# A gather kernel on one core: four gathers a round cut short by 1, 2, 4 and 9 rows, SyncE fetching the rows left over

## The reference

```
h    = relu(layernorm(x))
cat  = concatenate(h[src], h[dst], edge_attr)          # E x 384
msg  = relu(cat @ W1 + b1)                             # W1: 384 x 128
aggr = segment_sum(msg, dst, N)
out  = x + layernorm(aggr + h) * gamma + beta
```

## Time and profile before

| | |
|---|---|
| median of three runs | 1979.93 us |
| profiled execution | 1981.21 us |
| its span, first to last instruction | 1979.4 us |
| busy: PE, GpSimd (POOL), ACT, DVE | 1568.1, 1486.8, 1315.3, 860.4 us |
| mean granted TensorE clock, as a share of 2.4 GHz | 0.903 |
| data moved | 305.82 MB, 155 GB/s |

### The profile page before, as it was taken

One profiled execution on the slowest core, in us unless ns is written; L12 is line 12 of the kernel. 1 busy time (PEld: TensorE's weight loads), 2 busy tenths in 40 slices (PEclk: granted clock), 3 DMA queues, 4 the chain that ended last, 5 costly groups with the idle time before them and its releaser, 6 DMA issues.

```text
span 1979.4 us, 51290 instructions
## 1 busy us (share of the span) xinstructions
PE 1568.1 (79%) x11881; PEld 1485.0 (75%) x11881; DVE 860.4 (43%) x3031; ACT 1315.3 (66%) x2288; POOL 1486.8 (75%) x1575
## 2 busy tenths in 40 slices
PE   5677888878888887888888778888878787877876
PEld 4577787877777787777777777778777677777766
DVE  6534444444444444444444444444344343434434
ACT  5566767667676666767676676767666676666655
POOL 7777777777777777777777777777777777777775
PEclk9888988889898888998888899889899998999998
DMA  9744645555454555555555555555555555555553
GB/s 247 203 135 141 172 139 162 151 154 158 141 171 143 160 155 148 166 139 165 148 155 157 147 166 144 158 154 157 152 146 151 149 150 151 158 146 151 145 158 86
DMA packets 244448, 305.82 MB, mean 155 GB/s; under 512 B 50892, under 2 KB 143540, under 8 KB 244420
## 3 DMA queue, kind: packets, MB, share of 16 engines
q1 hardware_dynamic: 168596, 192.06, 31.9%
q0 software_dynamic: 50048, 102.60, 20.4%
q10 hardware_dynamic: 25776, 10.86, 1.9%
HBM read 281.68 MB, written 23.64 MB: 154 GB/s over the span
## 4 chain that ended last, share of the span: by engine, by line
POOL 30%; issue 23%; DMA 20%; PE 13%; DVEq 7%; DVE 4%; POOLq 1%; ACT 1%; ACTq 0%
POOL a_rows L524 27%; DMA a_rows<-table_a,picks 20%; DVEq L1225 5%; PE ps_pre L678 4%; PE ps_pre L679 4%; POOL aggr L500 3%; PE ps_edge L665 2%; DVE msg L1221 2%; PE ps_sum L690 1%; PE ps_sum L697 1%; DVEq L1218 1%; DVE e_norm L1253 1%; ACT space L894 0%; DVEq L1220 0%; PE ps_fin L690 0%
## 5 line engine op out<-in xcount | busy, mean ns | idle before, releaser
L524 POOL DMA_INDIRECT a_rows<-table_a,picks x1500 | 1417.1, 945 | 457.0 <-issue 402.5
L678 PE MATMUL ps_pre<-w_c,edge_cols 128*128 128x128 f32 x3128 | 680.6, 303 | 60.2 <-issue 39.6
L679 PE MATMUL ps_pre<-b_win,onehot_cols 128*128 128x128 f32 x3128 | 670.7, 300 | 0.0
L1221 DVE TENSOR_TENSOR msg<-ps_pre,a_rows 128x512 f32<-128x512 f32 x391 | 270.2, 691 | 874.1 <-DMA a_rows<-table_a,picks 640.3
L907 ACT ACTIVATE msg<-msg 128x512 f32<-128x512 f32 x391 | 246.2, 630 | 603.1 <-DVE msg L1221 587.0
L678 PEld LDWEIGHTS ps_pre<-w_c,edge_cols 128*128 128x128 f32 x3128 | 538.8, 216 | 83.5 <-ACT edge_cols L900 63.3
L679 PEld LDWEIGHTS ps_pre<-b_win,onehot_cols 128*128 128x128 f32 x3128 | 540.2, 216 | 0.0
L894 ACT ACTIVATE space<-space,base_all 64x512 f32<-64x512 int32 x391 | 474.1, 1213 | 13.3 <-issue 10.1
L690 PE MATMUL ps_sum<-onehot,msg 128*128 128x64 f32 x1568 | 225.2, 291 | 105.8 <-ACT e_rows L925 54.9
L690 PEld LDWEIGHTS ps_sum<-onehot,msg 128*128 128x128 f32 x1568 | 212.5, 210 | 125.0 <-ACT e_rows L925 65.5
L902 ACT ACTIVATE onehot_cols<-space,ones 64x512 f32<-64x512 f32 x391 | 277.4, 709 | 0.0
(11 more groups left out here) (123 smaller groups left out, 1032.8 us busy)
## 6 DMA issues: line engine op xcount, KB each, us to landing
edges<-in_edge_attr SPq DMA_DIRECT2D x391, 256.0 KB
space<-in_dst SPq DMA_DIRECT2D x391, 128.0 KB
a_rows<-table_a,picks POOLq DMA_INDIRECT x1500
b_win<-table_b SPq DMA_DIRECT2D x391, 32.0 KB
out<-out_rows SPq DMA_DIRECT2D x97, 64.0 KB
table_b<-b_rows ACTq DMA_DIRECT2D x96, 64.0 KB
x_all<-in_x SPq DMA_DIRECT2D x13, 448.0 KB, 6.8
table_a<-a_out SPq DMA_DIRECT2D x13, 448.0 KB
```

Of the source, the lines that this page charges most:

```text
L524: pool.indirect_dma_start(a_rows[:, u, k, :], None, table_a[:, :], bass.IndirectOffsetOnAxis(ap=picks[:, u, k:k + 1], axis=0),).then_inc(s ...
L678: pe.matmul(to, edge_cols[:, u % 2, k * P:(k + 1) * P], w_c[:, :], start=True, stop=False)
L679: mm = pe.matmul(to, onehot_cols[:, u % 2, k * P:(k + 1) * P], b_win[:, u, :], start=False, stop=True)
L1221: dve.tensor_tensor(msg[:, u % 2, :, :].rearrange("p k f -> p (k f)"), ps_pre[u % 2][:, :], a_rows[:, u, :, :].rearrange("p k f -> p (k f) ...
```

## The change

In the first group of each round (u = 0) the four gathers take the first 127, 126, 124 and 119 partitions in place of 128. The 1 + 2 + 4 + 9 = 16 rows left over are fetched by SyncE, each with a transfer of one row of 512 B from table_a whose row number stands in a register. The row numbers are loaded from src into hand_ids in the first phase (round r in partition r), DVE copies them by the four places into hand_picks (16 numbers a round, one partition per round), and SyncE reads them into eight registers at a time (BATCH): eight behind the loads of the round's first group, eight behind those of its second. Ahead of the first eight it waits for the add of the first group of the round before, which frees a_rows[:, 0]. DVE's add of the first group waits for the 16 rows by a semaphore of their own. The second branch of the kernel isn't touched.

```diff
+GATHERED = (127, 126, 124, 119)
+BATCH = 8
...
+    HAND_FROM = min(GATHERED)
+    HAND_AT = [(p, k) for k in range(SUB) for p in range(GATHERED[k], P)]
+    HAND = len(HAND_AT)
...
             load_ids(0, src)
+            sp.dma_start(hand_ids[0:ROUNDS - 1, :, :],
+                         src[0:(ROUNDS - 1) * UNROLL * GROUP].rearrange(
+                             "(r e) -> r e", r=ROUNDS - 1)[:, HAND_FROM * SUB:GROUP].rearrange(
+                             "r (p k) -> r p k", k=SUB)).then_inc(s_hand_ids, 16)
...
+                def fetch(i, batch):
+                    _, rows = nc.values_load_multi_w_load_instructions(
+                        bass.at_runtime_partition(hand_picks[0:1, batch * BATCH:(batch + 1) * BATCH], i),
+                        [mybir.EngineType.SP], min_val=0, max_val=N - 1, skip_runtime_bounds_check_because="src holds node numbers")
+                    for n in range(BATCH):
+                        p, k = HAND_AT[batch * BATCH + n]
+                        sp.dma_start(a_rows[p:p + 1, 0, k, :], table_a[bass.ds(rows[n], 1), :]
+                                     ).then_inc(s_hand_rows, 16)
+
+                def fetches(i, u):
+                    if u == 0 and past(i, 1):
+                        sp.wait_ge(s_z, (i - 1) * UNROLL + 1)
+                    if u < HAND // BATCH:
+                        fetch(i, u)
+
+                sp.wait_ge(s_hand_picks, SUB)
                 for i in range(3):
                     for u in range(UNROLL):
                         step(i, u)
+                        fetches(i, u)
 
                 def round_(i):
                     for u in range(UNROLL):
                         step(i, u)
+                        fetches(i, u)
                     sp.wait_ge(s_out, i - 2)
...
                     for k in range(SUB):
+                        n = GATHERED[k] if u == 0 else P
                         pool.indirect_dma_start(
-                            a_rows[:, u, k, :], None, table_a[:, :],
-                            bass.IndirectOffsetOnAxis(ap=picks[:, u, k:k + 1], axis=0),
+                            a_rows[0:n, u, k, :], None, table_a[:, :],
+                            bass.IndirectOffsetOnAxis(ap=picks[0:n, u, k:k + 1], axis=0),
                         ).then_inc(s_a_rows[u][k], 16)
...
+            dve.wait_ge(s_hand_ids, 32)
+            at = 0
+            for k in range(SUB):
+                n = P - GATHERED[k]
+                dve.tensor_copy(hand_picks[0:ROUNDS, at:at + n],
+                                hand_ids[0:ROUNDS, GATHERED[k] - HAND_FROM:, k]).then_inc(s_hand_picks, 1)
+                at += n
...
+                    if u == 0:
+                        dve.wait_ge(s_hand_rows, (i + 1) * (HAND * 16))
```

More of the change, by code:

```diff
@@ L154, in build @@
         b_rows = sb("b_rows", [P, H])
+        hand_ids = sb("hand_ids", [P, P - HAND_FROM, SUB], I32)
+        hand_picks = sb("hand_picks", [P, HAND], I32)
         early_picks = sb("early_picks", [P, EARLY_GROUPS, SUB], I32)
@@ L269, in build @@
         s_first_picks = sem("s_first_picks")
+        s_hand_ids = sem("s_hand_ids")
+        s_hand_picks = sem("s_hand_picks")
+        s_hand_rows = sem("s_hand_rows")
         s_early_picks = sem("s_early_picks")
@@ L388, in _ @@
             load_ids(0, src)
+            sp.dma_start(hand_ids[0:ROUNDS - 1, :, :],
+                         src[0:(ROUNDS - 1) * UNROLL * GROUP].rearrange(
+                             "(r e) -> r e", r=ROUNDS - 1)[:, HAND_FROM * SUB:GROUP].rearrange(
+                             "r (p k) -> r p k", k=SUB)).then_inc(s_hand_ids, 16)
+            last = (ROUNDS - 1) * UNROLL * GROUP
+            sp.dma_start(hand_ids[ROUNDS - 1:ROUNDS, :, :],
+                         src[last + HAND_FROM * SUB:last + GROUP].rearrange("(o p k) -> o p k", o=1, k=SUB)
+                         ).then_inc(s_hand_ids, 16)
             with sp.Fori(0, CHUNKS // 2 - 1 - X_LEAD) as pair:
@@ L455, in _ @@
                     step(ROUNDS - 1, u)
+                    fetches(ROUNDS - 1, u)
                 for b in range(ROUNDS - 4, BLOCKS):
```

## The result

The changed kernel takes **2215.68 us** (median of four runs, 2210.56 to 2218.13); the kernel before, beside it, 1979.86 us (four runs). The ratio is 1.119, 95% interval 1.1175 to 1.1203: 236 us slower. The forecast was 2167 us, slower by SyncE. What follows is of the profiled execution, 2210.56 us with a span of 2208.7.

What follows compares the result with a forecast made beforehand. GpSimd's gathers were taken as the bound; SyncE, with 7.1 us free a round and 9.2 added, would take over. Start 76.3, unrolled rounds 56.4, 94 rounds 2000.3, then the tail: 2166.1 span, forecast 2167 us, range 1962 to 2450.

Steps and rivals of the forecast that it cites:

- What bounds the kernel, and SyncE's room: Main loop: GpSimd's gathers run end to end, 1873 of 1979 us; SyncE has 7.1 us of each round to give.
- Sixteen fetches: SyncE's one-row transfers: 0.48 us each, 7.7 us a round, or 0.66 and 10.6 with b_win's issue.
- Loads of eight registers: SyncE's two row-number loads: 0.45 us for the instruction, 0.76 a load, 1.5 a round; bounds 1.2 and 4.9.
- one by one: Rival on SyncE's register loads: each register costs a full 0.268 us, 12.6 us a round, 2495 us; chance 0.10 (2390 to 2495).
- the sum: SyncE's round: 12.1 us of old work plus 9.2 of new makes 21.3, giving 2167 us for the kernel.
- The landing and the wait for the add: Arrival of shortened gathers, 2 to 3 us late inside 5.2 spare, and SyncE's wait for DVE's add: both cost nothing.
- The shortened gathers: GpSimd's 392 gathers with fewer rows: time goes by rows, saving 11.6 us; bounds nothing to 15.3 us.
- the rule on divisors: Gathers' landing: a transfer uses the largest number of engines up to 16 dividing its slowest dimension; the sum stays the same.
- The bound against: GpSimd's shortened gathers: an odd shape could cost at most 0.12 us more each, 47 us over 392 gathers.
- odd sizes cost more: Rival on GpSimd: odd gather sizes cost more than the rows save, SyncE keeping up; 2027 us, chance 0.05.
- SyncE binds, GpSimd wants 19.06: Main loop: SyncE becomes the bound at 21.3 us a round where GpSimd needs only 19.06.
- the likeliest case's own range: Whole kernel: SyncE binds with register loads near one trip, 2100 to 2230 us; chance 0.38.

Runs made afterwards that it cites:

- e6: The change with 8 rows a round: one gather of 120 rows, the others 128, one batch of eight fetches; 1988.39 us, ratio 1.0049.
- e8b: Kernel before, plus eight rows a round fetched into memory for 64 rounds, and four whole gathers left out in round 64; 1986.20 us, ratio 1.0035.
- e5: The change with all 16 fetched rows taken from one gather of 112 rows, the other three 128; 2171.81 us, ratio 1.0975.
- e2b: Kernel before with gathers of 127, 126, 124 and 119 rows and nothing fetched; 2192.61 us, ratio 1.1078.

## Why the prediction was right and where it was wrong

*What bounds the kernel, and SyncE's room.* Right. GpSimd end to end, and SyncE has 7.1 us a round to give: e6, with one batch, stays inside it; e8b, with 7.25 us, just doesn't.

*Sixteen fetches.* 0.48 us each was predicted, 0.42 measured ((3.17 - 0.225) / 7). L360's 0.286 us was the right neighbour and still too dear; the issue is 0.225. Two batches with their loads were to add 9.2 us. The block from b_win's start to the next edges is 4.89 and 4.77 us where it was 0.82: 8.0 together.

*Loads of eight registers.* 0.45 us was taken for the instruction, 0.552 measured. One register takes 0.268, so each of seven more adds (0.552 - 0.268) / 7 = 0.04 us. The rival "one by one" (2495 us) is out, and with it, for a load from SBUF, the 200 ns a register of the Trainium skill's "Runtime: NRT & Kernel Launch", section "Instruction fetch mechanics".

*What the sum lacked on SyncE:* the load of b_win's row number behind a batch takes 0.605 us in place of 0.268 (L438's median; half of its loads stand in a group that follows fetches), twice a round 0.3 us. That makes 8.7 us in place of 9.2. The predicted round was 21.3, e5's 21.24; predicted 2167 us, e5 2171.8. **As a forecast for SyncE's half the sum is right to 5 us**, with errors of half a microsecond a round that cancel: without the 8.7, e5's round has 12.5 us where the walk of a round gave 12.1. In the round shown above, for instance, the fourth group up to the next round's edges takes 3.93 us where the sum had 3.71.

*The landing and the wait for the add.* Right in the main: e2b's GpSimd has no stop at all, so no landing held up a gather; DVE waits 436 us for gathered rows where it waited 640 before. The wait for the add was put at nothing and is 18.8 us.

*The shortened gathers: the step that failed.* It said -0.12 us a round, by rows; measured are +2.13 (+2.17 with the two gathers behind). Two things were wrong. That a gather's time goes by rows: 64 rows cost what 128 do within 0.04 us, so there was no saving to be had from any cut. And the rule on divisors was applied to the landing alone: "by that rule the sum stays the same". It was taken for granted that GpSimd's own 0.945 us has nothing to do with how the transfer is split, though the trace had only sizes of 128 and so could not say. The bound against, 0.12 us a gather, was taken from L500, whose gathers all have 128 rows, so that their higher mean isn't a matter of size; the real price was 0.53 on the mean, over four times the bound. The rival "odd sizes cost more" (2027 us, chance 0.05) was the right mechanism with a price too low by far. Priced rightly it would have stood at 2193, beside the forecast.

*Where the two meet.* The forecast of 2167 came out 49 us low: e5, SyncE alone, is 2172; e2b, GpSimd alone, is 2193; both together 2216. So the step "SyncE binds, GpSimd wants 19.06" put its figure on the lower one of two bounds that stand close together: up to 1885 us GpSimd sets the pace, and only the last 17.6 us (23 by the medians) are SyncE's. The result lies in the likeliest case's own range (2100 to 2230) in part by luck: of the 209 us that were missing all but 44 are hidden, as they run beside SyncE's work.

*Signs that were named.* "Gathers of 127 rows far from 0.945 us" was listed among those that would show the prediction wrong, and it is what the trace has (2.55), as "SyncE rounds of about 21.3 without a hole" is there on the other side. "GpSimd with gaps over 0.30 us", named as a sign of being right, is there seven times only: that is the mark of the wrong bound.

*The clock.* The mean granted TensorE clock is 0.851 where it was 0.903, and PE is busy for 77 us longer. Nothing in the prediction spoke of it, and it is no rival for the cause: the gathers run with their 0.30 us gaps up to 1885 us, so up to there no wait for PE held them up.

## What to carry to other kernels

An indirect gather has a price per instruction, and rows left out of it save next to nothing. Keep its rows a multiple of 16, and save on it only by having fewer of them. By the pitches measured, 128 rows fetched one at a time cost another queue 128 x 0.42 = 54 us, and free 1.25 us here. When work moves from a bound queue to one with room, measure that room per round, keep below it, and price the changed instruction on both sides: here either half alone costs 10%.

## What the runs showed of the hardware

- A gather's time on GpSimd: about 0.95 us up to eight rows per part, then 0.0133 us for each row more in a part, where the number of parts is the largest divisor of the row count up to 16. Of the thirteen sizes measured 127 rows are the dearest, 2.55 us; one row more makes it 0.945.
- A one-row transfer with its row number in a register: 0.225 us of issue into SBUF at a fixed place, 0.42 from one to the next; 0.526 and 0.82 into memory with a second register in its address.
- A load of one register behind a batch of such transfers into SBUF takes 0.61 us in the median, otherwise 0.27 to 0.29. Behind e8b's batches, which go to memory, it takes 0.276. No run shows the cause.
- A fetch's issue just behind a gather of 127 rows: 0.54 us in the median for 0.225, in 40 cases of the changed kernel's trace.
- The same program took 1979 us on some chips and 2823 to 2836 (medians) on three others, with equal median durations of single instructions and waits in the sequencers that nothing in the profile ends. Only comparisons within one chip hold, and a half that is hidden on one can bind on the other: the short gathers cost 10.8% on a chip of the first kind and 0.8% on one of the second.
